# A fused two-block kernel on one core: one weight load between two others, a subtraction moved from GpSimd to VectorE, and the first unit's weights prepared a stage earlier

## The reference, cut to what matters

```
att   = softmax(gelu(gelu(cond @ W0 + b0) @ W1 + b1) @ W2 + b2)        # 32 x 8
y     = einsum('boi,bih->boh', einsum('bk,koi->boi', att, weight), x) + (att @ bias_k)[:, :, None]
u     = y @ kernel + bias + LoRA(y)      # a LoRA for each of 8 groups, and a shared one; rank 32
x     = x + u
c     = grouped conv1d(x, weight, K=9, groups=4) + (cond @ c_weight.T + fside)[:, :, None]
x1,x2 = split(c @ w12.T + b12)           # w12 is 2048 x 1024
x     = x + (silu(x1) * x2) @ w3.T + b3  # w3 is 1024 x 1024
```

## Time and profile before

| | |
|---|---|
| median of 3 runs | 794.06 us (793.2 to 794.22) |
| the profiled execution | 797.76 us, of which the span of its core 796.0 us |
| mean granted clock of PE | 0.995 |
| PE busy | 778.0 us (98%) |
| DVE, ACT, POOL busy | 523.1, 215.6, 81.7 us |
| base stage starts at full pace | about 71 us into the span |
| convolution | 273 to 331 us |
| gate units | 331 to 640 us |
| output units | 640 to 793 us |

### The profile page before, as it was taken

How to read it: one execution, slowest core, us unless ns; L and a number is a source line. 1 busy time by engine, 2 the same in 40 slices (tenths; PEclk the granted TensorE clock), 3 DMA queues, 4 the chain that set the end, 5 groups by cost and what they waited for, 6 DMA issues and landing times.

```text
span 796.0 us, 10457 instructions
## 1 busy us (share of the span) xinstructions
PE 778.0 (98%) x3933; PEld 659.6 (83%) x3933; DVE 523.1 (66%) x620; ACT 215.6 (27%) x254; POOL 81.7 (10%) x53
## 2 busy tenths in 40 slices
PE   7979999999999999989999999999999999999998
PEld 6867888888888899968888888888888888888886
DVE  4876646255353479987777759877765896555552
ACT  5541101001000032243333337333333731111110
POOL 2430351422313000000000000000000000000000
PEclk9999999999999999999999999999999999999999
DMA  8939665545475899244455134288862764444441
GB/s 228 312 142 269 151 158 130 132 113 145 116 169 123 181 277 235 80 133 132 133 147 157 40 130 135 79 230 236 238 245 81 253 223 159 166 174 161 158 174 64
DMA packets 90604, 131.47 MB, mean 165 GB/s; under 512 B 11048, under 2 KB 70296, under 8 KB 87624
## 3 DMA queue, kind: packets, MB, share of 16 engines
q1 hardware_dynamic: 87664, 130.72, 56.1%
q10 hardware_dynamic: 2792, 0.11, 0.2%
q0 software_dynamic: 112, 0.17, 0.1%
HBM read 79.24 MB, written 51.72 MB: 165 GB/s over the span
## 4 chain that ended last, share of the span: by engine, by line
PE 84%; DVE 7%; DMA 6%; SPq 2%; ACT 1%; issue 1%; DVEq 0%
PE ps L1823 37%; PE ps L1564 27%; PE ps L1883 19%; DMA raw<-in_L_ffn_kernel 3%; DVE cr L1268 2%; DVE cf L1274 1%; DVE cf L1260 1%; DMA a_scratch<-w_a_f 1%; DVE wk_lo L1055 1%; DVE c_st L1274 1%; DMA lora_b_scratch<-lb_c_lo 1%; DMA lb<-lora_bs_scratch 1%; DVE w_a_f L1218 1%; ACT wk_hi L803 1%; SPq L528 0%
## 5 line engine op out<-in xcount | busy, mean ns | idle before, releaser
L1823 PE MATMUL ps<-cr,w_s_hi 128*128 128x512 f32 x512 | 159.0, 392 | 2.5 <-ACT s L909 2.5
L1823 PE MATMUL ps<-cr,w_a_hi 128*128 128x512 f32 x384 | 118.4, 389 | 0.0
L1823 PEld LDWEIGHTS ps<-cr,w_s_hi 128*128 128x128 f32 x512 | 96.5, 189 | 23.5 <-issue 3.3
L1823 PE MATMUL ps<-cr,w_s_lo 128*128 128x512 f32 x256 | 100.3, 392 | 0.0
L1823 PEld LDWEIGHTS ps<-cr,w_a_hi 128*128 128x128 f32 x384 | 71.9, 188 | 15.1 <-issue 0.2
L1137 DVE TENSOR_TENSOR x_t<-ps,x_t 128x1024 f32<-128x1024 f32 x16 | 19.5, 1223 | 96.7 <-PE ps L1564 96.7
L1564 PE MATMUL ps<-wk_hi,y_hi 128*128 128x512 f32 x256 | 80.5, 395 | 0.7 <-DVE wk_lo L1055 0.5
L1564 PE MATMUL ps<-wk_lo,y_hi 128*128 128x512 f32 x256 | 79.0, 390 | 0.0
L1564 PE MATMUL ps<-wk_hi,y_lo 128*128 128x512 f32 x256 | 78.9, 389 | 0.0
L737 POOL TENSOR_TENSOR x_t<-x_in,f_bias 128x1024 f32<-128x1024 f32 x16 | 62.0, 3879 | 152.0 <-DMA x_scratch<-x_t 152.0
L1823 PE MATMUL ps<-cr,w_a_lo 128*128 128x512 f32 x192 | 74.7, 389 | 0.0
(11 more groups left out here) (173 smaller groups left out, 1251.8 us busy)
## 6 DMA issues: line engine op xcount, KB each, us to landing
x_scratch<-x_t SPq DMA_DIRECT2D x128, 64.5 KB, 2.2
x<-x_scratch SPq DMA_DIRECT2D x32, 258.0 KB, 6.9
x_in<-in_x SPq DMA_DIRECT2D x16, 512.0 KB, 6.7
r_scratch<-r_t SPq DMA_DIRECT2D x16, 512.0 KB, 3.3
h_scratch<-s SPq DMA_DIRECT2D x32, 256.0 KB, 2.3
h_f<-h_scratch SPq DMA_DIRECT2D x8, 1024.0 KB, 5.9
res<-r_scratch SPq DMA_DIRECT2D x16, 512.0 KB, 5.0
raw<-in_L_ffn_w SPq DMA_DIRECT2D x56, 128.0 KB, 4.4
```

What stands on the lines that cost most here:

```text
L1823: last = pe.matmul(o, l, r, start=first and q == 0 and n == 0, stop=q == 3 and n == 2, skip_group_check=True)
```

## The change

It touches three places.

1. First phase. `load_wk(5)` is issued between the two halves of LoRA B's loads. DVE makes `wk_lo` of all eight parts, part 0 ahead of `y_rest(0)`. POOL adds x and bias of tiles 0 and 1 only after `take_z(0)`. Part 5 is prepared ahead of the shared LoRA B's turn on ACT and DVE; on ACT part 6 goes behind `lb_hi_part(3)`. The waits on the first small loads get a semaphore for each load, and the taps' transposes are done in two halves.
2. Unit 0's weights. DVE turns them behind `take_z(7)` and sums them behind tile 14 in the base stage, into buffers of their own (`turn_0`, `sums_0`). Their store goes to ACT's queue, ahead of `s_hi(0)`. Three `c_sum` of the convolution are split in two halves of the rows.
3. Unit 1's weights are turned in the convolution, and unit 0 has an order of its own on ACT and DVE.

```diff
+        turn_0, sums_0 = at("turn_0", [P, 2, PH, P], 72), at("sums_0", [P, 4, 4, P], 80)
...
-        POOL_WK = (0,)
...
+        def turned_to(n):
+            return Af[prep_set(n)] if n else turn_0
+        def sums_to(n):
+            return Sf[prep_set(n)] if n else sums_0
+        def turned_w12(n):
+            return turned_to(n)[:, :, :, :].rearrange("p h q m -> p (h q m)")
...
             load_wk(4)
             load_lora_b(0)
+            load_wk(5)
             load_lora_b(1)
...
             store_bias(1, cb_c, cb_stored)
-            load_wk(5)
             load_wk(6)
             load_wk(7)
...
-            for t in range(6, 9):
+            for t in range(6, 10):
                 load_x8(t)
-            store_a(0)
-            load_x8(9)
...
-            for k in POOL_WK:
-                pool.wait_ge(wk_hi_made, k + 1)
-                pool.tensor_tensor(by_quarter(wk_lo[:, k, :]), in_quarters(raw[k % 4]), by_quarter(wk_hi[:, k, :]),
-                                   ALU.subtract).then_inc(wk_lo_pool, 1)
...
             pool.wait_ge(fbias_in, 16)
+            pool.wait_ge(z_taken, 1)
             for t in range(2):
                 pool.wait_ge(x_loaded[t], 16)
                 x_plus_bias(t, t)
...
             wk_hi_part(3)
             wk_hi_part(4)
+            wk_hi_part(5)
             act.wait_ge(lbs_mm, 1)
             act.activation(lbs_part(0).bitcast(F32R), lbs_turn, ACT.Copy).then_inc(lbs_made, 1)
-            wk_hi_part(5)
-            wk_hi_part(6)
             for n in range(4):
                 lb_hi_part(n)
+            wk_hi_part(6)
             wk_hi_part(7)
...
             a_hi(0, 0)
             a_hi(0, 1)
+            act.dma_start(a_dram[0], turned_w12(0)).then_inc(a_stored, 16)
             s_hi(0, 0)
             s_hi(0, 1)
...
-            act.wait_ge(c_taken, 8 + NB)
-            for u in range(HALF_UNITS - 1):
+            a_hi(1, 0)
+            part_copy(0, 0)
+            a_hi(1, 1)
+            part_copy(0, 1)
+            s_hi(1, 0)
+            s_hi(1, 1)
+            part_copy(0, 2)
+            silu(0, 0)
+            silu(0, 1)
+            for u in range(1, HALF_UNITS - 1):
                 gate_unit(u)
...
+            wk_lo_part(0)
             y_rest(0, 0, 0)
             add_bias(1)
             y_rest(1, 0, 1)
...
             wk_lo_part(4)
+            wk_lo_part(5)
             dve.wait_ge(lbs_made, 1)
             dve.tensor_tensor(lbs_part(1).bitcast(F32R), lbs_turn, lbs_part(0), ALU.subtract).then_inc(lbs_made, 1)
-            wk_lo_part(5)
             take_z(0, 0, True)
...
+            turn_w12(0, 0)
+            turn_w12(0, 1)
+            take_x1(14, 0)
+            residual(14, 0, 112)
+            weight_sums(0)
+            take_x1(15, 1)
+            residual(15, 1, 112)
...
+            def c_sum_rows(dst, a, b):
+                rows = [cf[n][:, 0:4, :].rearrange("p b e -> p (b e)") for n in (dst, a, b)]
+                dve.tensor_tensor(*rows, ALU.subtract).then_inc(c_rows_made, 1)
...
             take_c(0)
-            turn_w12(0, 0)
+            a_lo(0, 0)
             take_c(1)
+            a_lo(0, 1)
             take_c(2)
-            turn_w12(0, 1)
+            s_lo(0, 0)
             take_c(3)
-            take_c(4)
-            weight_sums(0)
-            take_c(5)
-            take_c(6)
-            s_lo(0, 0)
-            take_c(7)
             s_lo(0, 1)
-            take_c(8)
-            a_lo(0, 0)
-            take_c(9)
-            a_lo(0, 1)
-            take_c(10)
+            for b in range(4, 8):
+                take_c(b)
+            dve.wait_ge(a_stored, 16)
+            dve.wait_ge(w_lo_made, 4)
+            for b in range(8, 11):
+                take_c(b)
+            c_lo_part(0, HI_A["b11"], LO_A["b11"], 1)
...
             take_c(28)
-            c_lo_part(LO_A["t3"], HI_A["t3"], LO_A["t3"], 4)
-            for b in range(29, NB):
-                take_c(b)
+            turn_w12(1, 0)
+            take_c(29)
+            take_c(30)
+            turn_w12(1, 1)
+            take_c(31)
             c_lo_part(10, HI_A["b22"], LO_A["b22"], 7)
             c_lo_part(LO_A["t4"], HI_A["t4"], LO_A["t4"], 6)
...
-            for u in range(HALF_UNITS - 1):
-                if u:
-                    hidden_a(u - 1)
+            weight_sums(1)
+            part_add(0, 0)
+            s_lo(1, 0)
+            a_lo(1, 0)
+            a_lo(1, 1)
+            s_lo(1, 1)
+            part_add(0, 1)
+            part_add(0, 2)
+            hidden_b(0)
+            for u in range(1, HALF_UNITS - 1):
+                hidden_a(u - 1)
...
-            turn_taps()
+            turn_taps(0)
...
             la_part(0, 0, 4)
+            turn_taps(1)
```

More of the change, by code:

```diff
@@ L819, in _, with take_taps @@
                            ACT.Copy).then_inc(las_hi_made, 1)
[L820 to L824, removed]
+            def take_taps(half):
+                act.wait_ge(taps_mm, half + 1)
+                act.activation(taps[:, :, half, :].rearrange("p g (q o) -> p g q o", q=PH),
+                               bank(6 + half).rearrange("p (q g o) -> p g q o", q=PH, g=GRP), ACT.Copy).then_inc(taps_made, 1)
+            take_taps(0)
             act.wait_ge(mix_zeroed, 1)
@@ L882, in s_hi @@
                 act.wait_ge(ws_made, 4 * n + 3 + part)
-                act.activation(Shi[s][:, two], Sf[s][:, two], ACT.Copy).then_inc(w_hi_made, 1)
+                act.activation(Shi[s][:, two], sums_to(n)[:, two], ACT.Copy).then_inc(w_hi_made, 1)
             a_hi(0, 0)
             a_hi(0, 1)
+            act.dma_start(a_dram[0], turned_w12(0)).then_inc(a_stored, 16)
             s_hi(0, 0)
@@ L1207, in _ @@
             take_z(7, 1)
[L1208 to L1211, removed]
             def turn_w12(n, half):
                 dve.wait_ge(w_in[half], 64 * (n + 1))
-                dst = Af[prep_set(n)][:, half]
+                dst = turned_to(n)[:, half]
                 dve.transpose(dst.rearrange("p q (m b) -> p q m b", m=4),
@@ L1240, in s_lo @@
                 dve.wait_ge(w_hi_made, 4 * n + 3 + part)
-                dve.tensor_tensor(Slo[s][:, two], Sf[s][:, two], Shi[s][:, two], ALU.subtract).then_inc(w_lo_made, 1)
+                dve.tensor_tensor(Slo[s][:, two], sums_to(n)[:, two], Shi[s][:, two], ALU.subtract).then_inc(w_lo_made, 1)
             def a_lo(n, half):
@@ L1254, in a_lo, with c_sum_rest @@
                 ins.then_inc(w_lo_made, 1)
-            sums = [0]
+            sums, first_sums = [0], [0]
+            def c_sum_rows(dst, a, b):
+                rows = [cf[n][:, 0:4, :].rearrange("p b e -> p (b e)") for n in (dst, a, b)]
+                dve.tensor_tensor(*rows, ALU.subtract).then_inc(c_rows_made, 1)
+                first_sums[0] += 1
+                dve.wait_ge(c_rows_made, first_sums[0])
+            def c_sum_rest(dst, a, b):
+                rows = [cf[n][:, 4:8, :].rearrange("p b e -> p (b e)") for n in (dst, a, b)]
+                dve.tensor_tensor(*rows, ALU.subtract).then_inc(c_sum_made, 1)
+                sums[0] += 1
+                dve.wait_ge(c_sum_made, sums[0])
             def c_sum(dst, a, b):
@@ L1624, in biases, with turn_taps @@
                 mm(bank(2)[0:NB, NC:2 * NC], emb_t[:, :], cw_t[:, :], True, True).then_inc(bias_mm, 1)
-            def turn_taps():
+            def turn_taps(half):
                 pe.wait_ge(wpad_made, 1)
-                for half in range(2):
-                    for q in range(PH):
-                        k0 = 8 + 8 * half - q
-                        last = pe.transpose(bank(6 + half)[:, q * NC:(q + 1) * NC],
-                                            wpad[:, k0:k0 + PH, :].rearrange("o k c -> o (k c)"), ident[0:NC, 0:NC])
+                for q in range(PH):
+                    k0 = 8 + 8 * half - q
+                    last = pe.transpose(bank(6 + half)[:, q * NC:(q + 1) * NC],
+                                        wpad[:, k0:k0 + PH, :].rearrange("o k c -> o (k c)"), ident[0:NC, 0:NC])
                 last.then_inc(taps_mm, 1)
@@ L1737, in _ @@
             y_tile(1, 1, 16)
-            pe.wait_ge(taps_made, 1)
+            pe.wait_ge(taps_made, 2)
             la_part(0, 4, 8)
```

77 lines of the change are left out of this document (40 added, 37 removed).

## The result

The changed kernel takes 790.48 us (median of 5 runs, 788.17 to 791.65), the kernel before 794.22 beside it: the ratio is 0.9944, with an interval of 0.9917 to 0.9971. So it is faster, by 0.3 to 0.8%. Forecast were 784.6 us and a range of 782.8 to 788.2. The direction was right, the time is above the range, and more than half of the 9.5 us is missing: 3.7 us came by the medians, 4.4 by the ratio.

A forecast was written before the change was run, and what follows sets the result against it. PE was taken as busy nearly all the time, so gains come only from its waits or lower-clock stretches. First phase 5.2 plus gate unit 0 4.3 made 9.5 us off 794.06: 784.6 us, range 782.8 to 788.2.

The forecast's parts named there:

- The sum: Whole kernel: gains of 5.2 and 4.3 us make 9.5, taken off the 794.06 us median to give 784.6.
- Term 1: First phase: PE's wait for z and the slow product behind it go; 6.0 or 4.5 us gained, taken as 5.2.
- I take 0: LoRA B's last load lands about 40.6, just when PE wants it: no wait, with a bound of 2.5 us.
- rival C: First phase: LoRA B's last load is 1 to 2.5 us late, total gain 7 to 8.5 us; chance 0.1.
- the later branch: First phase: `wk_lo(6)` waits for POOL's last cast, `wk_lo(7)` ends at 57.0, LoRA B's rows land at 65.9; gain 4.5 us.
- Term 2: Gate unit 0: PE's wait for ACT's copy and the slow clock behind it go, a gain of 4.3 us.
- DVE has taken batch 10 at 293.6 ... so 332.6: Convolution: DVE's remaining work, 39.0 us, was counted to reach the last take at 332.6.
- B (clock): First phase: the clock falls in the new wait for tile 3, total gain 7.7 us, time 786.4; chance 0.25.
- D (the wait in unit 0 stays): Gate unit 0: DVE is later than counted and holds PE up, only 5.2 us gained, 788.9; chance 0.07.
- E: First phase: z comes no earlier, PE waits about 2.7 us, that gain falls to 2.5 or less, 787.3; chance 0.07.
- F: First phase: LoRA B's loads land later than 50.2 and eat all gains, time above 794.06; chance 0.03.
- G: Both places: nothing changes, because the two waits have other causes than named; chance 0.03.

The follow-up runs named there:

- e1: The kernel before, unchanged, profiled and timed again: 795.36 us, ratio 1.001.
- e2: The changed kernel, unchanged, profiled and timed again: 790.27 us, ratio 0.9941 to the kernel before.
- e3: The kernel before with only the first-phase part of the change: 794.53 us, ratio 0.9993.
- e4: The kernel before with only the weights of units 0 and 1 and the new orders of the convolution and unit 0: 791.59 us, ratio 0.9959.
- e5: The changed kernel with one line moved, the sum for t4 ahead of the take of batch 20: 789.5 us, ratio 0.9922 to the kernel before.
- e9: The changed kernel with the small loads counted in two semaphores again: 791.1 us, ratio 0.9951 to the kernel before.
- e6: The kernel before with one wait added, POOL adding x and bias only behind `take_z`: 794.04 us, ratio 0.9985.
- e7: The kernel before with only weight part 5's load moved between LoRA B's loads: 794.35 us, ratio 0.999.
- e8: The changed kernel with weight parts 6 and 7 made ahead of z and tile 3 loaded ahead of LoRA B's stores: 793.29 us, ratio 0.9968 to before.
- e11: e5 with high halves of parts 6 and 7 and part 6's low half made earlier, POOL behind all DVE's subtractions: 788.32 us, ratio 0.9916 to before.
- e12: The edits of e10 and e11 together: 789.0 us, ratio 0.9926 to the kernel before.
- e10: e5 with part 5's load back behind LoRA B's loads, and ACT's and DVE's orders with it: 790.12 us, ratio 0.9935 to the kernel before.

## Why the prediction was wrong

**The sum: "nothing says that the two places differ in it; so 794.06 - 9.5".** This is the step that failed. The terms were read in an execution of 797.76 us and taken off a median of 794.06, with the 3.7 us between them unexplained. By e1 they were the long wait itself. Taken off its own execution the sum gives the 788.3 that the prediction names, and with the result at 790.48, 3.7 of the 5.9 us that it came out too low are this step. 2.2 us are left for the terms. Counted from the median instead, what the profiles show of the two terms is 0.8 + 3.1 = 3.9 us, and the measured gain is 3.7 (4.6 in e2). Of the prediction's own signs of being wrong two came: LoRA B's products began later than 41, and DVE's last work came after PE wanted it.

**Term 1, the first phase, 5.2 us.** Near right for the execution in which it was read: `u_lora` moved by 4.43 us from one profile to the other. As a typical value it was mis-sized. It measures 0.6 us by the times (e3; 1.4 by e2 against e4), and by the profiles some 0.8: 66.56 is the mean of e1 and e4, 65.72 that of the five with the new first phase (changed, e2, e3, e5, e9). The mechanism was right, POOL's additions in the way of DVE (e6, e7), but its price depends on where part 5's landing meets POOL's two additions.

**The start, "I take 0".** LoRA B's loads behind part 5 are late by a little, rival C in its mildest form: PE waits 0.34 us for them in e2, 0.54 in e5, 1.06 in e8. In the changed kernel's first profile the products begin at 42.45, after 0.47 us behind POOL's last cast, which took 2.20 us beside `wk_lo(5)`; some of the rest was lost at the start, where PE's 16 expert products took 3.68 us, against 3.23 in the kernel before. The bound of 2.5 held.

**The chain behind it.** The forecast had a wait of 2.2 to 2.4 us for tile 3 and none for LoRA B's rows. Measured are 0.88, since PE came later, and then 1.06 for the rows: SP issues them behind tile 3's load, from 57.59 on, and the last lands at 61.19 + 5.38 = 66.57, behind the 65.9 of the later branch. "LoRA B's way through DRAM doesn't bind" is wrong, and e11 shows it bare: 1.43 us for the rows and nothing for tile 3. `u_lora` at 65.0 to 66.5 was met all the same, but for 0.1 us.

**Term 2, gate unit 0, 4.3 us.** The price of the place was right, and more firmly than the prediction could know. In e3 and e7 PE waited there 2.90 + 1.42 and 3.01 + 1.43 us with the clock at 1.0; in the kernel before, 2.47 with a fall that cost 1.79. Either way it is 4.3 to 4.4: what the slow clock takes in one execution, a second wait takes in the other. What failed is "DVE has taken batch 10 at 293.6 ... so 332.6", the count of DVE's work without a wait: 59.4 us from the start of the convolution, where it took 63.3. The stall of 3.22 us is most of the 3.9. The slack of 1.2 to 1.9 was there, and took up what it could; the prediction says that with DVE 3 us late some of the wait comes back, and 1.27 + 0.45 did (0.47 + 0.42 in e2). The mean of the rest falls from 523.4 (before, e1, e3, e6, e7) to 520.3 (changed, e2, e4, e8, e9), by 3.1, and to 518.9 with the sum first, by 4.5. So some 1.4 of the 4.3 us were in that one order of two instructions.

**The rivals.** B (clock) came in e12 alone. D (the wait in unit 0 stays) was partly right in its cause, DVE later than counted, with a third of its price. E falls: z was never waited for in the new order, except in e8. F and G fall.

## What to carry to other kernels

Before a wait of one profiled execution is taken off a median, compare that execution's time with the median: an excess that nothing explains may be the wait. A second profile of the same kernel would have changed this forecast by 4 us, which is as much as the change was worth. And where an engine's work is counted up to a deadline, its waits for buffers that a store must free belong in the count, as soon as the edit packs that work closer.

## What was not expected of the hardware

The length of a wait doesn't tell whether the clock falls. In the same place it fell to 0.50 after 2.47 us (before), 2.67 (e6) and 2.69 (e1) and stayed at 1.0 after 2.90 (e3) and 3.01 (e7); for tile 3 it fell after 1.90 (e12) and not after 1.65 (e10). At the start the granted clock stands at 1.00 in the rows from 5 to 20 us, yet most of the expert products take 634 ns apiece in both kernels, the shortest of them 379 in the kernel before, and the first four of LoRA A's matmuls behind them 421 to 582 in the changed kernel, where the later ones take 275. Where the pace changes differs between executions. The Trainium skill (TensorE: Matmul & The Clock Gate, What's actually happening) says that the point at which PE reaches its full clock varies from run to run. These starts agree with it if the slow pace is the lower clock, which the granted clock of these rows doesn't show. It is one source of the spread in LoRA B's start: where the sixteen expert products take 3.19 to 3.25 us (before, e6, e7), LoRA B's begin at 40.54 to 40.67, and where they take 3.68 (e1, e4), at 41.27 and 41.33. What sets it wasn't tried.
